# A decoder layer on one core: LAG 7 to 8 in the scan, the first unit's row maxima in two halves, norms of batches 3 and 4 one unit later

## The chip, the core and the metric

One core of a Trainium2 chip computes everything. The metric is device time in microseconds (us) of one launch, as the median of the runs shown. PE is TensorE (PEld its weight loads), DVE VectorE, ACT ScalarE, POOL GpSimd, SP the engine that issues most DMAs.

## What is computed

`x` is four batches of 512 tokens with 256 features, in float32. Three blocks follow each other, each added to `x`:

```python
x = x + mamba(layernorm(x))              # 2 layers; D_INNER 512, 16 states
x = x + cross_attention(layernorm(x), ctx)   # 16 heads of 16, 512 keys
x = x + ffn(layernorm(x))                # shared expert + top 2 of 8
```

A layer of the first block projects to 512 inner channels, runs a convolution of 4 taps and a scan over time with 16 states per channel, and sums the states times C:

```python
v = BETA * v + mi_t
h = dA_t * h + v
y_t = einsum('ben,bn->be', h, C_t)
```

The attention subtracts each query's maximum before the exponential, divides by the sum and projects. The experts follow it and are not touched here.

## The kernel before

**The scan stage.** Two layers of four batches make eight passes, k = 0 to 7, of 64 steps each (16 states by 4 tiles of 128 channels). A step i is one scan of 128x512 on DVE (line 911), which needs its decay from ACT (`dA`, line 1067) and its input from PE (line 704, `v`; PE writes the inputs of two steps at once, at each even step, into two adjoining banks of PSUM). POOL then multiplies the result by C (line 1140), and PE adds it to the sum of its channel tile by four transposes (line 681, `pe_add_state`). PE does this addition LAG steps later: in step i it writes the inputs (if i is even), and then adds state i - LAG. `LAG` is 7 (line 255), and there are LAG + 2 buffers for the states. So PE, in order, can write inputs only when POOL is through with an earlier state.

After its 16th state a channel tile's sum is copied by ACT (line 974, "y"), transposed by PE (line 664, "bt"), combined on DVE (line 828, "xd") and gated on POOL (line 1099). `plan_mid` (line 455) and `plan_back` (line 436) put these pieces at steps that are counted from LAG, while `plan_front` (line 395) puts the pieces of the next pass (projections "p" and "z" line 576, "xp" 586, "dbcT" 595, "d" 600, transposes "u" 614, chunk ends "e1" to "e3" 641) at fixed steps. The convolution's taps are three instructions on DVE (line 799).

**Banks.** Inputs and pieces share six banks (NRING). `banks_for` (line 59) goes through them in PE's order: a piece takes the bank that was used longest ago, an input pair the two adjoining ones used longest ago. PE waits until the bank's last content is read, by a scan (semaphore `scan_done`), by DVE (`bank_dve`) or by ACT (`bank_act`). So which wait stands ahead of an input pair follows from where the pieces stand.

**The attention stage.** It has eight units u (two per batch, 8 heads each) of 16 slots s. Slot s: PE writes the scores of a key tile and two heads into a pair of banks (line 1449, and line 1453 adds the negated maxima by a matmul with `nrow`), ACT takes the exponential of 128x1024 (line 1517), and PE multiplies by the values (line 1470) once for two slots. The maxima themselves come from scores the other way round: PE line 1433, DVE line 1584, 16 of them for each unit. They run four slots ahead (`maxima_at`, line 1328, one per slot). After a unit's 16th maximum `dve_max_parts` (line 1586) splits them in two parts, PE turns them into rows ("rows", line 1400) and DVE copies the rows (line 1562). Scores, maxima and the pieces of `opening` (line 1321) share three pairs of banks in turn; all other pieces ("v", sums, norm, "xn", "q", "out", rows) share a single bank (NONE = 1, line 1289).

`opening` runs ahead of unit 0: the transposes and queries of batch 2 ("xn" line 1386, "q" 1391), unit 0's maxima 4 to 15 (0 to 3 are made earlier), its rows, and maxima 0 to 3 of unit 1. The values "v" of batch 1 (line 1396) are made in slots 0 and 1 of unit 0. Unit 0 also holds, on DVE, the residual sum of batch 3 (`dve_add_x(2)`, line 879), the statistics of batches 3 and 4 (lines 149, 156) and batch 3's scaling (line 171), and on ACT their square root (line 162), for which ACT loads a table and then the exponential's again. Batch 3's "xn" and "q" stand in slots 3, 4, 6 and 8 of unit 1.

## Time and profile before

| | us |
|---|---|
| median of 3 runs | 1496.05 |
| lowest, highest | 1495.28, 1501.35 |
| profiled execution | 1499.4 |
| its span, first to last instruction | 1498.1 |
| 64 steps of the scan stage, 488.80 to 599.50 | 110.7 |
| first to last start of an exponential in attention | 989.4 to 1244.3 |

The stretches of the second group of rows end at the first score of a unit or slot: opening before 988.13, unit 0 from there to 1031.24 (slot 2 starts at 999.71, 6 at 1006.26, 10 at 1014.29), unit 1 to 1063.30; unit 5 is 1165.56 to 1194.09. A busy time is followed by the number of instructions in brackets. A timeline row gives start, duration, engine, line, operation, output<-input, count, and in brackets the idle time ahead of it with the instruction that ended it. Rows of neighbouring instructions are merged. TensorE's granted clock is given as a share of 2.4 GHz: 1.00, or 0.50 for 1.2 GHz. Times in the text are those of the trace's axis, from the start of the span.

### The profile page before, as it was taken

How to read it: one execution, taken by the hardware profiler on the slowest of the kernel's cores; microseconds unless marked ns; L12 is line 12 of the kernel's file. 1: busy time of each engine (PE TensorE's matmuls, PEld its weight loads, DVE VectorE, ACT ScalarE, POOL GpSimd, SP SyncE). 2: the span in 40 equal slices, each digit the busy share in tenths (PEclk: the TensorE clock that was granted, in tenths of full speed). 3: DMA queues.
4: the chain of work that ended last, by engine and by line, in shares of the span. 5: the costliest groups of instructions: out<-in, count | busy, mean ns of one | idle time of the engine just before them, and what ended most of it. 6: DMA issues, size and time to landing. Idle time of an engine off the chain costs nothing.

```text
span 1498.1 us, 47021 instructions
## 1 busy us (share of the span) xinstructions
PE 1365.4 (91%) x20570; PEld 966.3 (65%) x20570; DVE 1054.5 (70%) x1345; ACT 891.2 (59%) x1303; POOL 939.7 (63%) x834
## 2 busy tenths in 40 slices
PE   6999999999999999999999988778998887999997
PEld 3567767767777777776776767433434343589996
DVE  4798788788788788888887888576777751522224
ACT  4767766776776776776776756126565564434440
POOL 1289989889989989989989988540422000044541
PEclk9999999999999999999999999869999999999999
DMA  6322221221321222122122336470725003412215
GB/s 228 148 101 87 87 87 59 87 87 59 115 87 62 84 88 82 63 88 87 62 84 87 111 127 157 94 137 11 131 43 99 0 2 113 177 58 70 70 62 186
DMA packets 44043, 137.38 MB, mean 92 GB/s; under 512 B 9024, under 2 KB 21952, under 8 KB 35008
## 3 DMA queue, kind: packets, MB, share of 16 engines
q1 hardware_dynamic: 37024, 117.85, 24.3%
q0 software_dynamic: 6816, 16.53, 5.0%
q8 instruction: 164, 2.69, 0.7%
q14 instruction: 39, 0.32, 0.1%
HBM read 108.00 MB, written 15.86 MB: 83 GB/s over the span
## 4 chain that ended last, share of the span: by engine, by line
PE 47%; DVE 27%; ACT 12%; issue 9%; DMA 3%; POOL 3%; DVEq 0%; SPq 0%; ACTq 0%; POOLq 0%
DVE hst L911 12%; PE psum L704 7%; PE psum L681 4%; PE psum L1470 4%; PE psum L1878 4%; PE psum L1890 4%; DVE overlay L799 4%; DVE w_early L911 3%; ACT dA L1067 3%; PE psum L641 3%; PE psum L1449 2%; ACT pT L1517 2%; PE psum L576 2%; DMA overlay<-x_hat,origin 2%; PE psum L1433 2%
## 5 line engine op out<-in xcount | busy, mean ns | idle before, releaser
L1140 POOL TENSOR_TENSOR hst<-hst,cb 128x512 f32<-128x512 f32 x399 | 511.2, 1304 | 89.1 <-DVE hst L911 87.1
L911 DVE TENSOR_TENSOR_SCAN hst<-dA,psum 128x512 f32<-128x512 f32 x399 | 464.0, 1203 | 100.8 <-PE psum L704 100.7
L681 PE MATMUL psum<-ident,hst 128*128 128x128 f32 x1596 | 236.9, 282 | 8.1 <-ACT xraw L974 3.6
L1067 ACT ACTIVATE dA<-delta,alog 128x512 f32<-128x512 f32 x256 | 178.1, 718 | 86.6 <-DVE hst L911 67.6
L1067 ACT ACTIVATE dA<-xres,alog 128x512 f32<-128x512 f32 x256 | 176.7, 718 | 69.2 <-DVE hst L911 52.0
L681 PEld LDWEIGHTS psum<-ident,hst 128*128 128x128 f32 x1596 | 174.8, 142 | 57.0 <-issue 20.5
L1584 DVE TENSOR_REDUCE nmax<-psum 128x2 f32<-128x1024 f32 x124 | 150.1, 1221 | 52.6 <-PE psum L1433 51.6
L1517 ACT ACTIVATE pT<-psum 128x1024 f32<-128x1024 f32 x128 | 126.9, 1024 | 92.9 <-PE psum L1453 91.7
L704 PE MATMUL psum<-filt,uT 64*64 64x86 f32 (+1 forms) x6144 | 144.5, 238 | 23.3 <-DVE hst L911 11.5
L704 PEld LDWEIGHTS psum<-filt,uT 64*64 64x64 f32 x6144 | 123.6, 133 | 58.4 <-issue 46.3
L704 PE MATMUL psum<-filt,c_early 64*64 64x86 f32 (+1 forms) x6144 | 143.9, 237 | 18.6 <-DVE hst L911 11.1
L704 PEld LDWEIGHTS psum<-filt,c_early 64*64 64x64 f32 x6144 | 123.2, 133 | 55.7 <-issue 41.7
L1140 POOL TENSOR_TENSOR w_early<-w_early,cb 128x512 f32<-128x512 f32 x113 | 145.7, 1302 | 18.8 <-DVE w_early L911 18.1
L911 DVE TENSOR_TENSOR_SCAN w_early<-dA,psum 128x512 f32<-128x512 f32 x113 | 133.4, 1203 | 32.7 <-PE psum L704 32.7
L2123 POOL DMA_INDIRECT overlay<-x_hat,origin x39 | 37.9, 972 | 185.8 <-DVE c_early L2069 174.2
L576 PE MATMUL psum<-overlay,w_early 128*128 128x512 f32 x256 | 122.6, 606 | 2.8 <-DVE w_early L911 2.0
L2129 POOL DMA_INDIRECT y_choice<-yb,goal x39 | 38.6, 989 | 70.4 <-DVE yb L2083 70.4
L1968 ACT ACTIVATE ht<-psum 128x512 f32<-128x512 f32 x39 | 23.3, 597 | 94.2 <-PE psum L1878 94.2
L1878 PEld LDWEIGHTS psum<-xt,xn 128*128 128x128 f32 x624 | 75.6, 192 | 3.0 <-DVE xt L2075 0.9
L1878 PE MATMUL psum<-xt,xn 128*128 128x128 f32 x624 | 76.1, 275 | 0.7 <-DVE xt L2075 0.7
L799 DVE SCALAR_TENSOR_TENSOR overlay<-psum,w_cv,overlay 128x509 f32<-128x509 f32 (+2 forms) x96 | 71.1, 743 | 6.9 <-ACT overlay L952 4.7
L1890 PE MATMUL psum<-w_down,ht 128*128 x312 | 73.7, 380 | 0.0
(251 smaller groups left out, 2110.8 us busy)
## 6 DMA issues: line engine op xcount, KB each, us to landing
cb<-c_rows SPq DMA_DIRECT2D x64, 1024.0 KB, 4.8
qk_first<-w_early SPq DMA_DIRECT2D x64, 64.0 KB, 2.6
w_up<-up_dram SPq DMA_DIRECT2D x8, 512.0 KB, 7.6
w_down<-down_dram SPq DMA_DIRECT2D x8, 512.0 KB, 13.6
w_up<-y_choice SPq DMA_DIRECT2D x8, 512.0 KB, 7.4
k_kept<-uT SPq DMA_DIRECT2D x3, 1024.0 KB, 5.9
v_kept<-xbs SPq DMA_DIRECT2D x6, 512.0 KB, 2.6
qk<-k_kept SPq DMA_DIRECT2D x48, 64.0 KB, 3.5
```

Of the source, the lines that this page charges most:

```text
L576: i = pe.matmul(bk, w_in[:, kt, m8 * P:(m8 + 1) * P], xnT[:, kt, :], start=kt == 0, stop=kt == KD - 1)
L681: m = pe.matmul(psum[:, Y0 + et % EP, t * P:(t + 1) * P], hst(i)[:, t * P:(t + 1) * P], ident[:], start=n == 0 and t == 0, stop=n == NSTAT ...
L704: m = pe.matmul(halves_at[half][e0:e0 + MT, :, t0:t0 + width], uT[k % 2][r0:r0 + KT, c, et * P + e0:et * P + e0 + MT], filt[r0:r0 + KT, f ...
L799: i = dve.scalar_tensor_tensor(out=dst, in0=bk[:, 0:S - late], scalar=w_cv[:, l, j, tap:tap + 1], in1=dst, op0=ALU.mult, op1=ALU.add)
L911: dve.tensor_tensor_scan(hst(i), a, v, 0.0, ALU.mult, ALU.add).then_inc(scan_done, 1)
L1067: act.activation(dA[:, a % NDA, :], delta[k % 2][:, et, :], ACT.Exp, scale=alog[:, k // B, et, n:n + 1]).then_inc(decay_done, 1)
L1140: pool.tensor_tensor(h, h, cb[:, q % 2, state_of(i)[1] % GN, :], ALU.mult).then_inc(g_done, 1)
L1470: m = pe.matmul(psum[i * HROW:(i + 1) * HROW, PV, :], vt[:, cp, kv, c0:c0 + HROW], pT[:, (m0 + i // 2) % NPT, i % 2, :], start=kv == 0, st ...
L1517: act.activation(pT[:, m % NPT], pair(u, "score", s), ACT.Exp, scale=HDIM ** -0.5).then_inc(pair_act, 1)
L1584: dve.tensor_reduce(nmax[:, u % 2, t, 2 * j:2 * j + 2], pair(u, "max", r), AX.X, ALU.max, negate=True).then_inc(pair_dve, 1)
L1878: m = pe.matmul(psum[:, U0 + j % NUB, ft * P:(ft + 1) * P], wu[:, j % NWU, kt * F + ft * P:kt * F + (ft + 1) * P], xt[:, j % NXT, kt, :], ...
L1890: m = pe.matmul(out_bank(j)[:, 0:D], ht[:, j % NHT, ft, :], w_down[:, bass.ds(at + ft * D, D)], start=ft == 0, stop=ft == FT - 1)
```

## The change

`LAG` becomes 8 (and the state buffers 10). The pieces y, bt, xd and the gates that are counted from LAG come one step later; those of `plan_front` stay. In attention, unit 0's maxima are turned into rows twice: maxima 0 to 7 in the opening (into `nrow[1]`), 8 to 15 in unit 0 (rows at slot 4, used from slot 8 on). The opening ends after maximum 9. Slots 0 to 9 of unit 0 hold two maxima each, all later slots one, so that from the end of unit 0 on they are four slots ahead as before. The residual sum, statistics, root and scaling of batches 3 and 4 go from unit 0 to unit 1 (slots 0 to 6), and batch 3's "xn" and "q" from slots 3, 4, 6, 8 of unit 1 to 7, 8, 10, 12.

```diff
@@ -252,7 +252,7 @@
-            NDA, AHEAD, LAG, NRING, Y0 = 5, 4, 7, 6, 6
+            NDA, AHEAD, LAG, NRING, Y0 = 5, 4, 8, 6, 6
...
@@ -1309,7 +1309,7 @@
-                    for s, name in zip((3, 4, 6, 8), project(b + 2)):
+                    for s, name in zip((7, 8, 10, 12) if u == 1 else (3, 4, 6, 8), project(b + 2)):
...
@@ -1319,23 +1319,27 @@
             opening = project(1)[:2]
-            for r in range(NMX, NSLOT):
+            HALF = NSLOT // 2
+            for r in range(NMX, HALF):
                 opening += [(0, "max", r)] + project(1)[r - NMX + 2:r - NMX + 3 if r - NMX < 2 else 0]
-            opening += [(0, "rows", 0)] + [(1, "max", r) for r in range(AHEAD)]
+            opening += [(0, "max", HALF), (0, "rows", 0), (0, "max", HALF + 1)]
+            to_come = [(0, r) for r in range(HALF + 2, NSLOT)] + [(u, r) for u in range(1, NU) for r in range(NSLOT)]
+            AT_ONCE = [2] * 10 + [1, 1] + [1] * AHEAD
+            slot(0, 4, 0, "rows", 1)
...
             def maxima_at(u, s):
-                if s < NSLOT - AHEAD:
-                    return (u + 1, s + AHEAD) if u + 1 < NU else None
-                return (u + 2, s + AHEAD - NSLOT) if u + 2 < NU else None
+                if u == 0:
+                    return to_come[sum(AT_ONCE[:s]):sum(AT_ONCE[:s + 1])]
+                at = sum(AT_ONCE) + (u - 1) * NSLOT + s
+                return to_come[at:at + 1]
...
-                    if maxima_at(u, s):
-                        v, r = maxima_at(u, s)
+                    for v, r in maxima_at(u, s):
...
@@ -1395,7 +1399,7 @@
-                    pe.wait_ge(max_lo, x + 1)
+                    pe.wait_ge(max_lo, x + 2 if x else j + 1)
...
@@ -1434,6 +1438,9 @@
+            def nrow_at(u, s):
+                return 1 if u == 0 and s < NSLOT // 2 else u % 2
...
@@ -1444,13 +1451,15 @@
+                elif (u, s) == (0, NSLOT // 2):
+                    pe.wait_ge(*taken(u, "rows", 1))
...
-                    m = pe.matmul(o[:, e, :], pick[k0:k0 + KR, j, :], nrow[k0:k0 + KR, u % 2, :], start=False, stop=True, tile_position=(k0, 0))
+                    m = pe.matmul(o[:, e, :], pick[k0:k0 + KR, j, :], nrow[k0:k0 + KR, nrow_at(u, s), :], start=False, stop=True, tile_position=(k0, 0))
...
@@ -1535,7 +1544,7 @@
-                        if s == 9 and u == 0:
+                        if s == 4 and u == 1:
                             act_ln_root(LN2[2], 2 * TB, NT)
...
@@ -1583,16 +1592,17 @@
-            def dve_max_parts(u):
+            def dve_max_parts(u, n, c0, c1):
...
+                dve.wait_ge(*taken(u, "max", 2 * c1 - 1))
+                dve.tensor_copy(hi, maxima).then_inc(max_hi, 1)
+                dve.wait_ge(max_hi, n + 1)
+                dve.tensor_tensor(lo, maxima, hi.bitcast(F32), ALU.subtract).then_inc(max_lo, 1)
...
@@ -1609,8 +1619,8 @@
+                        if (x, j) == (0, HALF - 1):
+                            dve_max_parts(0, 0, 0, HALF // 2)
...
@@ -1618,23 +1628,25 @@
+                        for x in maxima_at(u, s):
+                            dve_max(*x)
+                            if x == (0, NSLOT - 1):
+                                dve_max_parts(0, 1, HALF // 2, UH)
...
+                            dve_max_parts(u + 1, u + 2, 0, UH)
...
+                        if s == 0 and u == 1:
                             dve_add_x(2)
...
+                        if s in (1, 2) and u == 1:
                             dve.wait_ge(x1_done, B)
...
+                            dve_ln_stats(LN2[2], (s + 1) * TB, (s + 2) * TB, xres, s == 2)
+                        if s == 3 and u == 1:
                             dve_ln_aggr(LN2[2], 2 * TB, NT)
...
+                        if s == 6 and u == 1:
                             dve_ln_rec(LN2[2], 2 * TB, NT)
                             dve_ln_scale(LN2[2], 2 * TB, 3 * TB, xres, True)
```

Three places of the order follow. In all, `psum` is the bank written, and the semaphores in brackets are what the instruction waits for.

**PE, last pass (k = 7), around its steps 38 to 40.** `hst` is a state buffer, `filt` and `uT` make a scan's input, `xraw` is the copied sum. Before:

```order
L704 MATMUL psum<-filt,uT 64x2x43 [waits scan_done]
L704 MATMUL psum<-filt,uT 64x2x43 x15
L704 MATMUL psum<-filt,uT 64x2x42 x8
L681 MATMUL psum<-ident,hst 128x128 [waits g_done]
L681 MATMUL psum<-ident,hst 128x128 x3
L681 MATMUL psum<-ident,hst 128x128 [waits y_out,g_done]
L681 MATMUL psum<-ident,hst 128x128 x3
L664 MATMUL psum<-ident,xraw 128x128 [waits y_out,scan_done]
L664 MATMUL psum<-ident,xraw 128x128 x3
L704 MATMUL psum<-filt,uT 64x2x43 [waits scan_done,filt_done]
```

Now:

```order
L681 MATMUL psum<-ident,w_early 128x128 [waits g_done]
L681 MATMUL psum<-ident,w_early 128x128 x3
L704 MATMUL psum<-filt,uT 64x2x43 [waits scan_done,filt_done]
L704 MATMUL psum<-filt,uT 64x2x43 x15
L704 MATMUL psum<-filt,uT 64x2x42 x8
L681 MATMUL psum<-ident,hst 128x128 [waits y_out,g_done]
L681 MATMUL psum<-ident,hst 128x128 x3
L664 MATMUL psum<-ident,xraw 128x128 [waits y_out,scan_done]
L664 MATMUL psum<-ident,xraw 128x128 x3
```

The addition that waits for ACT's copy (`y_out`) stood ahead of the input pair of steps 40 and 41, and stands behind it now.

**PE, pass k = 3, steps 48 to 50**, with the transposes "u" (L614). Before:

```order
L704 MATMUL psum<-filt,uT 64x2x43 [waits scan_done,bank_act,filt_done]
L704 MATMUL psum<-filt,uT 64x2x43 x15
L704 MATMUL psum<-filt,uT 64x2x42 x8
L681 MATMUL psum<-ident,w_early 128x128 [waits g_done]
L681 MATMUL psum<-ident,w_early 128x128 x3
L614 MATMUL psum<-ident,overlay 64x64 [waits u_done,scan_done,bank_act]
L614 MATMUL psum<-ident,overlay 64x64 x31
L681 MATMUL psum<-ident,hst 128x128 [waits g_done]
L681 MATMUL psum<-ident,hst 128x128 x3
L704 MATMUL psum<-filt,uT 64x2x43 [waits scan_done]
```

Now:

```order
L704 MATMUL psum<-filt,uT 64x2x43 [waits bank_act,filt_done]
L704 MATMUL psum<-filt,uT 64x2x43 x15
L704 MATMUL psum<-filt,uT 64x2x42 x8
L681 MATMUL psum<-ident,hst 128x128 [waits g_done]
L681 MATMUL psum<-ident,hst 128x128 x3
L614 MATMUL psum<-ident,overlay 64x64 [waits u_done,scan_done]
L614 MATMUL psum<-ident,overlay 64x64 x31
L681 MATMUL psum<-ident,hst 128x128 [waits g_done]
L681 MATMUL psum<-ident,hst 128x128 x3
L704 MATMUL psum<-filt,uT 64x2x43 [waits bank_act]
```

The two input pairs waited for a scan, and now wait for copies of ACT alone. Odd passes (1, 3, 5) have this order; in the even ones (2, 4, 6) the pair of step 48 still waits for the scan before it.

**DVE, from the end of the mamba stage to slot 2 of unit 0.** TENSOR_REDUCE is a maximum, `nsplit` the parts, `nrow` the rows, `vt` the values. Before:

```order
L1584 TENSOR_REDUCE nmax<-psum 128x2
L1549 SCALAR_TENSOR_TENSOR part<-psum,b_qk,part 128x512
L1584 TENSOR_REDUCE nmax<-psum 128x2 x10
L1593 CAST nsplit<-nmax 128x8x8
L1595 TENSOR_TENSOR nsplit<-nmax,nsplit 128x8x8
L1609 CAST pick<-pT 128x512
L1562 CAST nrow<-psum 128x512
L1584 TENSOR_REDUCE nmax<-psum 128x2 x5
L1557 TENSOR_TENSOR vt<-psum,b_v 128x16x16 x2
```

Now:

```order
L1593 TENSOR_REDUCE nmax<-psum 128x2
L1558 SCALAR_TENSOR_TENSOR part<-psum,b_qk,part 128x512
L1593 TENSOR_REDUCE nmax<-psum 128x2 x2
L1603 CAST nsplit<-nmax 128x8x4
L1605 TENSOR_TENSOR nsplit<-nmax,nsplit 128x8x4
L1593 TENSOR_REDUCE nmax<-psum 128x2
L1619 CAST pick<-pT 128x512
L1571 CAST nrow<-psum 128x512
L1593 TENSOR_REDUCE nmax<-psum 128x2 x3
L1566 TENSOR_TENSOR vt<-psum,b_v 128x16x16 x2
```

The first rows stood behind ten maxima in a row, and stand behind three now.

## Rows read from the trace of the kernel before

**Rows 1.** Page: engines' shares of the chain; the value products (busy us, mean ns).

```profile
PE 47%; DVE 27%; ACT 12%; issue 9%; DMA 3%; POOL 3%; DVEq 0%; SPq 0%; ACTq 0%; POOLq 0%
...
L1470 PE MATMUL psum<-pT,vt 128*32 128x512 f32 x512 | 69.7, 627 | 3.2 <-ACT pT L1517 3.2
```

**Rows 2.** Stretches: length, busy PE, PEld, DVE, ACT, POOL; PEclk, DMA share, GB/s.

```profile
488.80:599.50 110.70, 104.92 (x2204) 79.45 (x2207) 92.65 (x95) 79.07 (x128) 99.94 (x82) 1.00 0.22 80
...
977.00:988.10 11.10, 6.06 (x20) 2.65 (x18) 9.99 (x13) 0.00 (x0) 11.09 (x24) 0.50 1.07 133
988.13:999.71 11.58, 10.55 (x28) 5.82 (x28) 5.83 (x7) 2.05 (x2) 2.22 (x1) 0.58 1.03 239
999.71:1006.26 6.55, 5.71 (x41) 2.42 (x40) 5.15 (x5) 3.88 (x4) 0.00 (x0) 1.00 0.18 55
1006.26:1014.29 8.03, 5.91 (x44) 2.25 (x40) 8.03 (x22) 4.10 (x4) 0.00 (x0) 1.00 0.00 0
1014.29:1031.24 16.95, 13.61 (x81) 5.73 (x77) 11.03 (x17) 9.50 (x10) 0.00 (x0) 0.80 0.00 1
1031.24:1063.30 32.06, 29.98 (x198) 13.22 (x194) 23.01 (x25) 19.92 (x23) 10.12 (x22) 1.00 0.48 77
...
1165.56:1194.09 28.53, 25.00 (x181) 11.35 (x178) 21.71 (x23) 17.39 (x19) 0.00 (x0) 1.00 0.00 1
```

**Rows 3.** Timeline of PE, pass k = 3: input pairs of steps 42 to 50.

```profile
471.92 1.12 PE L704 MATMUL psum<-filt,uT 64*64 64x86 f32 x48 [0.60 <-DVE w_early L911]
...
475.17 1.12 PE L704 MATMUL psum<-filt,uT 64*64 64x86 f32 x48 [1.10 <-DVE xbs L828]
...
483.94 1.12 PE L704 MATMUL psum<-filt,uT 64*64 64x86 f32 x48 [0.36 <-DVE hst L911]
...
487.66 1.12 PE L704 MATMUL psum<-filt,uT 64*64 64x86 f32 x48 [0.33 <-DVE w_early L911]
```

**Rows 4.** Timeline, pass k = 4: an addition waits for POOL; ACT meanwhile.

```profile
502.53 0.42 PEld L681 LDWEIGHTS psum<-ident,hst 128*128 128x128 f32 x4 [0.85 <-POOL hst L1140]
...
501.35 1.95 ACT L1067 ACTIVATE dA<-delta,alog 128x512 f32<-128x512 f32 x3
503.32 1.75 ACT L1029 COPY c_early<-psum 16x512 f32<-16x512 f32 x3
```

**Rows 5.** Timelines of PE and DVE, last pass: waits for POOL, ACT and PE.

```profile
864.10 0.66 PE L681 MATMUL psum<-ident,w_early 128*128 128x128 f32 x4 [1.22 <-POOL w_early L1140]
...
906.03 1.08 PE L681 MATMUL psum<-ident,hst 128*128 128x128 f32 x4 [3.63 <-ACT xraw L974]
...
909.76 1.22 DVE L911 TENSOR_TENSOR_SCAN hst<-dA,psum 128x512 f32<-128x512 f32 x1 [2.54 <-PE psum L704]
```

**Rows 6.** Timelines of DVE and ACT: the opening of attention and the first exponential.

```profile
971.76 11.40 DVE L1584 TENSOR_REDUCE nmax<-psum 128x2 f32<-128x1024 f32 x10
...
984.98 0.69 DVE L1562 CAST nrow<-psum 128x512 fp32r<-128x512 f32 x1 [0.94 <-PE psum L1400]
...
989.39 1.02 ACT L1517 ACTIVATE pT<-psum 128x1024 f32<-128x1024 f32 x1 [18.33 <-PE psum L1453]
```

**Rows 7.** Timelines of ACT and PE around the root in unit 0.

```profile
1015.03 1.28 ACT L162 ACT_TABLE_LOAD   x1
...
1019.03 0.80 PE L1433 MATMUL psum<-qk_first 64*128 64x512 f32 x2 [3.10 <-ACT pT L1517]
...
1022.66 0.80 PE L1449 MATMUL psum<-qk_first 64*128 64x512 f32 x2
...
1024.11 0.63 PE L1449 MATMUL psum<-qk_first 64*128 64x512 f32 x2
```

**Rows 8.** Timeline of DVE: residual sum, statistics, a query part.

```profile
1005.13 1.22 DVE L879 TENSOR_TENSOR xres<-xres,xm 128x1024 f32<-128x1024 f32 x1
...
1007.39 1.39 DVE L149 BATCH_NORM_STATS2 stat<-xres 128x6 f32<-128x256 f32 x4
...
1045.75 0.75 DVE L1549 SCALAR_TENSOR_TENSOR part<-psum,b_qk,part 128x512 fp32r<-128x512 f32 x1 [1.49 <-ACT part L1504]
```

27 lines of the change are left out of this document (7 added, 20 removed).

## The prediction

> **What bounds the kernel now.** I read the page first, then the chain of waits, then stretches. The page says that no engine alone is the bound: the chain lies 47% on PE, 27% on DVE, 12% on ACT and only 3% on POOL [rows 1]. That already says something on LAG: a later addition gives POOL more time, and POOL is almost never what is last. In one pass of 110.7 us PE is busy for 104.9, DVE for 92.7 and POOL for 99.9 [rows 2]; PE and DVE hand the chain to and fro through the six banks. The places where PE waits for DVE ahead of an input pair are in [rows 3], the one where it waits for POOL in each pass is in [rows 4]. Attention: in the opening the first exponential comes after ACT was idle for 18.33 us, while DVE makes ten maxima in 11.40 us [rows 6]. PE is busy for 6.06 of 11.10 us there, at a granted clock of 0.50, so 1.2 GHz [rows 2]. The units that follow are bound by PE: unit 5, which has no projection, takes 28.53 us, or 3.57 for two slots; unit 1 with a projection takes 32.06 [rows 2].
>
> **Part 1, LAG 8: the waits for POOL.** PE waits 0.85 us for POOL once a pass. With LAG 8 that wait goes, since POOL is then asked for the state before. But ACT is in one row of work at that time, without a gap, from 501.35 on [rows 4], and DVE's next scans wait for ACT's decays: the wait is hidden, and I take 0 for it (bounds 0 and -0.85 for each of 7 passes, -6). In the last pass POOL is really last, since two gates and filters stand in its queue; PE waits 1.22 us [rows 5]. What PE needs next, the output projection, needs the last gate, which POOL now does one state later than before, so POOL's end there does not move. Only one addition of PE (0.66) goes out of its way: -0.5.
>
> **Part 2, LAG 8: other banks for the input pairs.** This is the part that counts. Since bt and xd move by a step and the fixed pieces don't, `banks_for` hands the banks out differently. Working its rule through for the six full passes:
> - Odd passes (1, 3, 5). Before, the pairs of steps 42, 48 and 50 need the scan just before them, and step 44's needs DVE's xd. PE waits 0.60, 0.36, 0.33 and 1.10 us there, 2.39 together [rows 3]. Now the pair of 42 needs a copy of ACT, 44's an xd two steps back, and 48's and 50's copies of ACT (the second place of the order). All of it could go, -2.4. DVE is only partly idle there, and the stretch after it hangs on ACT's copies of u and e1, so I take -1.5 (bounds -2.4 and 0).
> - Even passes (2, 4, 6). Step 44 no longer waits for xd, but for scan 43, and 46 and 48 wait as before; 50 waits for ACT only. That is worth -0.3 to -0.6; I take -0.5.
> - In all six, xd of channel tile 2 now stands behind a scan more, and the pair of step 10 waits for it: +0.2 by counting DVE's row (a scan of 1.22 [rows 5] against PE's 1.12 for a pair [rows 3]), bounds 0 and +0.6.
>
> Sum: 3 x -1.5 + 3 x -0.5 + 6 x 0.2 = -4.8.
>
> **Part 3, LAG 8: the last pass.** At step 39 PE adds the first state of a channel tile and waits 3.63 us for ACT's copy; the input pair of step 40 stands behind it, and DVE is idle for 2.54 us [rows 5]. Now the pair stands ahead (first place of the order), so these 2.54 us go. ACT's copy comes one decay (1.95 / 3 = 0.65 [rows 4]) later, which the two scans in hand cover. I take -2.5 (bounds -3 and 0). After that POOL runs without a gap to the end of the stage, and it had been waiting for DVE before, so it can start earlier by as much.
>
> **Part 4, the opening.** Before, the rows are copied at 984.98 [rows 6]. Now maxima 6 to 8 stand ahead of them instead of 6 to 15. Three maxima at 1.14 (11.40 / 10) from 971.76 are over at 975.2; parts and the copy of `pick` come between, as before: from the last maximum's end, 983.2, to the rows' end, 985.7, it was 2.5; one of the three maxima now falls into the wait in it, which saves 0.8. So the rows are done at 975.2 + 2.5 - 0.8 = 976.9. PE's first score was also behind four maxima of unit 1, and started at 988.1; now it stands directly behind the rows and maximum 9, at 977.0. -11.1 us (bounds -10 and -11.5).
>
> **Part 5, unit 0.** The ten maxima that left the opening are in slots 0 to 9.
> - Slots 0 and 1 took 11.58 us at clock 0.58, with the four products that make the values through the one bank [rows 2]. One more maximum each is about 0.3 of a slot's 1.45 at 1.2 GHz [rows 7], so 0.4: +0.9, together 12.5.
> - Slots 2 to 9. The nearest stretch without other work, slots 2 to 5, takes 6.55 for four slots, 3.28 for two [rows 2]. With four maxima for two slots DVE alone needs 4.56, and because PE's value products (69.7 / 64 = 1.1 for two slots [rows 1]) stand in order between a maximum and the next score, I take 4.86 (an estimate; bounds 4.56 and 5.4). Times 4, and 1.0 for parts and rows: 20.5. Slots 10 to 15 have one maximum: as in unit 5, 11.9.
> - Together 44.9 us, against 43.1 before (988.13 to 1031.24): +1.8. It would be more, but the work that leaves unit 0 had cost there: in slots 6 to 9, 8.03 us instead of 6.55, and from slot 10 on 16.95 instead of 11.9 (root, and the clock at 0.80 behind it) [rows 2, 7].
>
> **Part 6, unit 1.** It took 32.06 us at clock 1.00 [rows 2]. Added are:
> - on DVE 1.22 (sum), 2 x 1.39 (statistics) [rows 8], and by estimate from these some 0.6 (aggregation) and 1.6 (reciprocal, scaling). In slots 0 to 3 that is 4.6 on top of four maxima of 1.14 and one group's sums: 9.5 or less for DVE where PE needs 4 x 28.53 / 16 = 7.1 by unit 5: +2.0.
> - on ACT the root between two table loads of 1.28. PE waited 3.10 behind them in unit 0 [rows 7], and will in unit 1: +3.0, with 2.5 more if the clock falls behind it as it did there (that is in the bounds).
> - "xn" of batch 3 in slot 7 waits for the scaling that ends in slot 6: +0.8. "q" in slots 10 and 12 now has sums (11) and rows (13) directly behind it on the single bank, which is free only after ACT's part and DVE's; DVE's takes 0.75 after a wait of 1.49 for ACT's [rows 8]. Two maxima and scores of cover leave +0.6 each, 1.2.
> - less 0.6, as DVE catches up while PE waits for ACT.
>
> Sum +6.4 (bounds +3 and +9). Of the queues: strips of batch 3 leave SP and POOL some 8 us later, and are first needed in slot 12 of unit 3, 60 us later: 0. ACT's root also waits for DVE's aggregation one slot before, as before.
>
> **The sum.** Mamba: -0.5 - 4.8 - 2.5 = -7.8. Attention: -11.1 + 1.8 + 6.4 = -2.9. Together -10.7 against the profiled 1499.4 us (span 1498.1), so about 1488.7 for a profiled run. The median of the runs is 3.4 below that run: 1496.05 - 10.7 = 1485.4.
>
> **A rule that speaks against it.** In slots 6 to 9 of unit 0 PE is busy for only 5.91 of 8.03 us and keeps the clock at 1.00; from 1014.29 on it is 0.80 on average, behind a wait of 3.10 us [rows 2, 7]. The Trainium skill, "TensorE: Matmul & The Clock Gate", section "A second HAM failure mode: psum-queue depth-cycling", says that short idle times between groups of matmuls, as PSUM buffers are gone through in turn, are enough to make the clock go to and fro. Unit 0 will have just such idle times. By the row the sum stays; by the rule it is the third rival below.
>
> **The rivals.**
> - *Only the last pass and attention gain* (chance 0.24). What speaks for it: DVE is busy for 92.7 of 110.7 us in a pass, and after step 50 comes a chain over e1, e2 and e3 that ACT's copies set, so PE's waits may be mere slack. Then part 2 is 0 or +1: 1490 to 1493, with the last pass absorbed as well 1494.
> - *Attention gains more* (0.16). If the root's 3 us fall into the time in which DVE is behind anyway, and the clock comes up earlier since PE is dense from 975 on, unit 1 costs +3 and unit 0 takes 42: 6 less, 1479.
> - *The clock stays at 1.2 GHz in units 0 and 1* (0.06). For it: the idle times of about 0.7 us for two slots in slots 2 to 9, where PE waits for DVE. Against it: slots 6 to 9 at 1.00 [rows 2]. Price: score, its row and a maximum take 1.45 us [rows 7] instead of half of that, the value products 2.2 instead of 1.1 [rows 1]; that is 0.8 more for two slots where DVE is the bound, and 1.6 where PE is: some +9 in unit 0 and +12 in unit 1, 1506 in all, slower than before. It decides if the clock stays down for more than 13 slots; as long as it falls only behind the root, as now, it is in the sum.
> - *The change doesn't do what it says:* the scores could start at 977 and be held by something else. The banks in turn give every score of slots 0 to 9 the pair that the score before had, so it waits for that exponential. A round of score, exponential (1.02 [rows 6]) and two hand-overs is 2.3 us, below DVE's 2.4 for a slot. If it is above, +0.3 for each of 8 slots: 1488. That is within my case's range.
>
> **How the numbers follow.** My case has 0.50 (1481 to 1489), the rivals 0.24, 0.16 and 0.06, and 0.04 is left for something between (the LAG parts making the scan stage longer while attention gains, 1496 to 1500). The predicted time is my case's, 1485.4. The range takes in the first rival and most of the second: 1478 to 1495. A difference of 0.5%, 7.5 us, is about what a measurement of this kernel can tell from no change; faster by more than that is below 1488.6: 0.46 of my case and the second rival, 0.62. Slower than 1503.5: 0.04. Within: 0.34.
>
> **What would show it.** Passes k = 1, 3, 5 about 1.5 us shorter than the even ones, where they are equal now; no wait for DVE ahead of PE's pairs of 48 and 50. No idle DVE in the last pass ahead of the scan of step 40. The first exponential some 15.5 us after the opening's first instruction instead of 26.5 (989.39 on today's axis, 978.3 then, less what the mamba stage gains). Unit 0 near 45 us, bound by DVE, at clock 1.00 from slot 2 on; unit 1 near 38 us with PE waiting for ACT in slots 5 and 6. I am wrong if odd and even passes stay equal, if unit 0 is above 50 us, or if units 2 to 7 change at all, which nothing here should move.

## The result, and the profile after

The changed kernel takes 1487.65 us (median of 7 runs, 1486.05 to 1491.99), the one before 1496.05: a ratio of 0.9947, 95% interval 0.9928 to 0.9965, so 8.4 us faster where I had said 10.7. Its profiled run took 1486.92 us, with a span of 1485.6; the span is 12.5 shorter than that of before. The sum was nearly right, the terms were not: the full passes gained more and the last pass nothing, the opening gained more, and unit 1 lost almost twice what I had put down for it.

The page of the changed kernel: busy time of the engines, and the chain of waits by engine, beside [rows 1].

```profile
PE 1361.3 (92%) x20574; PEld 966.7 (65%) x20574; DVE 1055.1 (71%) x1348; ACT 892.2 (60%) x1303; POOL 938.6 (63%) x834
...
PE 50%; DVE 25%; ACT 11%; issue 8%; DMA 2%; POOL 2%; SPq 1%; DVEq 0%; ACTq 0%
```

SPq, the queue of SyncE, was at 0% of the chain before and is at 1% now; the last pass will show why. The stretches of the changed kernel (length, busy PE, PEld, DVE, ACT, POOL; granted clock, DMA share, GB/s): passes k = 3 and 4, the last pass up to attention's opening, the opening, unit 0 whole and in three parts, unit 1 whole and in four.

```profile
372.74:482.59 109.85, 104.95 (x2205) 79.71 (x2201) 92.82 (x95) 79.21 (x129) 99.98 (x82) 1.00 0.24 84
482.59:593.13 110.54, 104.83 (x2204) 79.58 (x2200) 92.72 (x95) 79.20 (x129) 99.92 (x82) 1.00 0.24 85
812.28:954.65 142.37, 127.35 (x2376) 99.95 (x2372) 111.90 (x122) 76.21 (x117) 113.60 (x93) 0.94 0.43 120
954.65:967.38 12.73, 8.99 (x34) 4.18 (x34) 8.67 (x12) 2.45 (x4) 9.25 (x13) 0.86 0.69 166
967.38:1009.33 41.95, 34.55 (x210) 16.09 (x210) 35.50 (x39) 16.65 (x17) 13.27 (x24) 0.96 0.60 114
967.38:977.67 10.29, 8.12 (x32) 5.01 (x32) 6.85 (x8) 2.05 (x2) 10.29 (x22) 0.84 1.06 154
977.67:997.46 19.79, 15.69 (x101) 6.42 (x101) 18.91 (x20) 8.20 (x8) 2.98 (x3) 1.00 0.71 161
997.46:1009.33 11.87, 10.74 (x82) 4.66 (x78) 9.74 (x12) 6.41 (x7) 0.00 (x0) 1.00 0.00 0
1009.33:1053.77 44.44, 35.33 (x196) 15.38 (x192) 28.66 (x47) 23.14 (x26) 9.56 (x20) 0.85 0.25 39
1009.33:1016.90 7.57, 4.41 (x30) 2.66 (x26) 6.53 (x11) 3.55 (x4) 0.00 (x0) 0.88 0.00 1
1016.90:1026.99 10.09, 8.05 (x42) 3.34 (x42) 5.50 (x15) 6.93 (x8) 0.00 (x0) 0.75 0.01 2
1026.99:1035.60 8.61, 6.53 (x30) 2.83 (x26) 4.78 (x8) 3.16 (x4) 4.08 (x8) 0.60 0.79 122
1035.60:1053.77 18.17, 16.34 (x99) 6.55 (x98) 11.84 (x15) 9.50 (x11) 5.48 (x12) 1.00 0.23 36
```

A pass is measured here from PE's first e1 product (step 50) to the same of the next. So read, the 12.5 us divide as follows: the opening of attention starts at 954.65 and not at 962.93 (-8.3), it lasts 12.73 to the first score and not 25.20 (-12.5), unit 0 41.95 and not 43.11 (-1.2), unit 1 44.44 and not 32.06 (+12.4), unit 2 33.67 and not 34.86 (-1.2), unit 6 +0.7, and what follows the last score is 2.6 shorter. That last item belongs to nothing: over all 14 profiled kernels of this study this part takes 250.7 to 256.4 us, in no relation to the edits. Unit 2's is no sure part either: nothing of it is edited, and it takes 33.7 us in five of the ten kernels with attention's change and about 35 in the other nine.

The same division for every kernel that ran (us, one profiled execution each; "scores" is the opening's start to the first score). The ratios are against the kernel before on the same chip, where its median was between 1495.9 and 1498.5, so kernels are compared by their ratios and not by their medians. Kernels that share a stage, such as the last passes of the change and of lag_alone, show how much one execution says of it.

| kernel | median | ratio (95%) | k = 3 | k = 4 | last pass | scores | unit 0 | unit 1 |
|---|---|---|---|---|---|---|---|---|
| before | 1496.05 | | 111.5 | 110.8 | 141.9 | 25.2 | 43.1 | 32.1 |
| the change | 1487.65 | 0.9947 (0.9928-0.9965) | 109.9 | 110.5 | 142.4 | 12.7 | 42.0 | 44.4 |
| lag_alone | 1487.48 | 0.9927 (0.9898-0.9956) | 109.2 | 110.5 | 142.5 | 25.4 | 43.3 | 32.1 |
| att_alone | 1497.95 | 0.9994 (0.9975-1.0014) | 111.2 | 110.8 | 141.9 | 13.9 | 43.6 | 43.3 |
| pieces_alone | 1487.01 | 0.9941 (0.9916-0.9967) | 109.7 | 110.7 | 143.8 | 25.5 | 43.3 | 32.1 |
| adds_alone | 1497.26 | 1.0007 (0.9989-1.0026) | 112.3 | 111.1 | 142.6 | 25.4 | 43.3 | 32.1 |
| aq_later | 1483.10 | 0.9899 (0.9867-0.9930) | 108.9 | 110.6 | 137.5 | 13.9 | 43.5 | 41.2 |
| ln_later | 1484.53 | 0.9911 (0.9880-0.9941) | 109.7 | 110.5 | 141.6 | 14.1 | 42.1 | 38.2 |
| halves_norms_back | 1484.33 | 0.9922 (0.9898-0.9946) | 108.6 | 110.5 | 142.4 | 12.7 | 51.2 | 32.1 |
| root_as_identity | 1484.62 | 0.9916 (0.9886-0.9946) | 109.7 | 110.5 | 141.9 | 12.7 | 43.5 | 40.5 |
| both_later | 1478.31 | 0.9883 (0.9859-0.9907) | 109.0 | 110.5 | 137.0 | 13.9 | 43.6 | 39.3 |
| even_as_odd | 1481.39 | 0.9890 (0.9858-0.9921) | 108.7 | 109.9 | 136.1 | 12.7 | 42.0 | 38.3 |
| xn_later | 1476.52 | 0.9868 (0.9838-0.9897) | 108.9 | 110.5 | 138.7 | 12.7 | 43.6 | 35.2 |
| even_last_bo | 1469.47 | 0.9822 (0.9791-0.9853) | 108.8 | 108.1 | 138.3 | 14.4 | 43.7 | 35.2 |

### The profile page after: what moved, and what is told of

It reads as the page before. It is cut to its first block, busy times and chain, and to the rows that moved or that the text cites. A ratio compares the mean times of both kernels' runs of the same rounds, so it can differ in the third digit from the quotient of the medians.

```text
span 1485.6 us, 47034 instructions
## 1 busy us (share of the span) xinstructions
PE 1361.3 (92%) x20574; PEld 966.7 (65%) x20574; DVE 1055.1 (71%) x1348; ACT 892.2 (60%) x1303; POOL 938.6 (63%) x834
## 4 chain that ended last, share of the span: by engine, by line
PE 50%; DVE 25%; ACT 11%; issue 8%; DMA 2%; POOL 2%; SPq 1%; DVEq 0%; ACTq 0%
DVE hst L911 11%; PE psum L704 7%; PE psum L681 5%; PE psum L1479 4%; PE psum L1890 4%; PE psum L1902 4%; DVE overlay L799 4%; ACT dA L1067 3%; PE psum L576 3%; DVE w_early L911 3%; PE psum L641 3%; PE psum L1458 2%; ACT pT L1526 2%; PE psum L1832 2%; DVE nmax L1593 2%
## 5 line engine op out<-in xcount | busy, mean ns | idle before, releaser
L1140 POOL TENSOR_TENSOR hst<-hst,cb 128x512 f32<-128x512 f32 x410 | 523.8, 1300 | 87.9 <-DVE hst L911 85.8
L911 DVE TENSOR_TENSOR_SCAN hst<-dA,psum 128x512 f32<-128x512 f32 x410 | 475.4, 1203 | 100.9 <-PE psum L704 100.9
L681 PE MATMUL psum<-ident,hst 128*128 128x128 f32 x1640 | 242.7, 283 | 5.1 <-ACT xraw L974 2.6
L681 PEld LDWEIGHTS psum<-ident,hst 128*128 128x128 f32 x1640 | 180.4, 142 | 55.9 <-issue 24.7
L1526 ACT ACTIVATE pT<-psum 128x1024 f32<-128x1024 f32 x128 | 127.0, 1024 | 84.9 <-PE psum L1462 83.1
L704 PE MATMUL psum<-filt,uT 64*64 64x86 f32 (+1 forms) x6144 | 145.1, 238 | 17.9 <-DVE hst L911 11.2
L704 PE MATMUL psum<-filt,c_early 64*64 64x86 f32 (+1 forms) x6144 | 143.5, 237 | 18.6 <-DVE hst L911 11.5
L1140 POOL TENSOR_TENSOR w_early<-w_early,cb 128x512 f32<-128x512 f32 x102 | 131.5, 1305 | 12.4 <-DVE w_early L911 11.7
L911 DVE TENSOR_TENSOR_SCAN w_early<-dA,psum 128x512 f32<-128x512 f32 x102 | 119.6, 1202 | 20.7 <-PE psum L704 20.7
L2141 POOL DMA_INDIRECT y_choice<-yb,goal x39 | 38.5, 986 | 68.2 <-DVE yb L2095 68.2
L1479 PE MATMUL psum<-pT,vt 128*32 128x512 f32 x512 | 71.8, 644 | 2.5 <-ACT pT L1526 2.5
```

The source lines that it names most:

```text
L681: m = pe.matmul(psum[:, Y0 + et % EP, t * P:(t + 1) * P], hst(i)[:, t * P:(t + 1) * P], ident[:], start=n == 0 and t == 0, stop=n == NSTAT ...
L704: m = pe.matmul(halves_at[half][e0:e0 + MT, :, t0:t0 + width], uT[k % 2][r0:r0 + KT, c, et * P + e0:et * P + e0 + MT], filt[r0:r0 + KT, f ...
L911: dve.tensor_tensor_scan(hst(i), a, v, 0.0, ALU.mult, ALU.add).then_inc(scan_done, 1)
L1140: pool.tensor_tensor(h, h, cb[:, q % 2, state_of(i)[1] % GN, :], ALU.mult).then_inc(g_done, 1)
L1479: m = pe.matmul(psum[i * HROW:(i + 1) * HROW, PV, :], vt[:, cp, kv, c0:c0 + HROW], pT[:, (m0 + i // 2) % NPT, i % 2, :], start=kv == 0, st ...
L1526: act.activation(pT[:, m % NPT], pair(u, "score", s), ACT.Exp, scale=HDIM ** -0.5).then_inc(pair_act, 1)
```

## Experiments 1 and 2: one half of the change alone

```
lag_alone, against before:
-            NDA, AHEAD, LAG, NRING, Y0 = 5, 4, 7, 6, 6
+            NDA, AHEAD, LAG, NRING, Y0 = 5, 4, 8, 6, 6
att_alone: the changed kernel with this line as before
```

> The kernel before with LAG = 8 and nothing else. Between the traces of before and after, the opening of attention starts 8.3 us earlier (962.93 to 954.65), and all of that should be LAG's: about 1488 us, odd passes (k = 1, 3, 5) 1.6 to 2.2 shorter than the 110.75 of before, even ones 0.2, the last pass (from its first L641 to the opening) unchanged near 142. Attention's units as before (43.1, 32.1). Rival: part of the 8.3 comes from what stands behind (code and data placed otherwise), then this kernel is at 1491 or above.

> The changed kernel with LAG = 7: attention's part of the change alone. By the traces of before and after: opening -12.5, unit 0 -1.2, unit 1 +12.4, unit 2 -1.2, so -2.4, and the opening's start at 962.9 as before: about 1493.5 us. Behind attention 2.6 us were also gone in the changed kernel; if they belong to attention's edits they show here too (1491), if to LAG's in the run of LAG alone, if in neither they are spread of one execution.

LAG alone gives all that was measured: 0.9927, with the passes of the changed kernel and attention as before. Attention's half gives nothing that can be measured, 0.9994: from the opening's start to the last score it takes 279.4 us against 280.3 before. The opening gained 11.3 and unit 1 gave back 11.2.

## Experiments 3 and 4: is it the banks or POOL?

LAG moves two things at once: PE's additions, and the pieces that the planner counts from LAG (y, bt, xd, output). Each can be moved alone. In pieces_alone all pairs and pieces stand in the very banks of the changed kernel, in adds_alone in those of before; for both this is exact: `banks_for`, given their orders, hands out the same banks pair for pair.

```
pieces_alone, against before:
-                    plan_back(k - 1, k, LAG - 2)
+                    plan_back(k - 1, k, LAG - 1)
-                    s = EP * NSTATE + LAG - 2 * EP + 2 + 2 * e
+                    s = EP * NSTATE + LAG + 1 - 2 * EP + 2 + 2 * e
adds_alone, against before: LAG = 8, and the two lines with LAG - 3 and LAG - 1
```

> The kernel before with PE's additions seven states later as they were, but y, bt, xd, gate and output pieces of plan_back and plan_mid one step later, where LAG = 8 puts them. The input pairs and pieces then have the very banks that LAG = 8 gives them. Theory (part 2 of the prediction): the scan stage gains by the banks, so odd passes (k = 1, 3, 5) are at 108.6 to 109.9 us and even ones at 110.5, as with LAG alone (108.63, 109.15, 108.64), and the whole is 1489 to 1491. Rival: the gain is that PE's additions no longer wait for POOL (0.85 us in each pass); then all passes stay at 110.75 and the whole at 1498.

> The kernel before with LAG = 8 for PE's additions alone: the pieces of plan_back and plan_mid stay at the steps, and all pairs and pieces in the banks, of LAG = 7. The counterpart of pieces_alone. By the theory passes stay at 110.75 and the whole is 1498 (the last pass 0 to -0.5); y of a channel tile may then wait one state for its last addition, up to +1 for each of the passes. By the rival the passes are at 109 to 110 each and the whole is near 1489.

The pieces carry the gain (0.9941), the later additions have none (1.0007) and cost 2.1 us over six passes. (The profiled run of pieces_alone is the slowest of its eight, 1495.99 us, so its trace shows less of the gain than the median does.) The timeline of PE in pass k = 3 shows where it comes from, pairs of steps 40 to 50. First pieces_alone, the pairs from step 42 on:

```profile
468.12 1.12 PE L704 MATMUL psum<-filt,uT 64*64 64x86 f32 x48
470.63 1.12 PE L704 MATMUL psum<-filt,uT 64*64 64x86 f32 x48
475.66 1.12 PE L704 MATMUL psum<-filt,uT 64*64 64x86 f32 x48
478.98 1.12 PE L704 MATMUL psum<-filt,uT 64*64 64x86 f32 x48
482.29 1.12 PE L704 MATMUL psum<-filt,uT 64*64 64x86 f32 x48
```

Then adds_alone, from step 40 on: the waits of [rows 3] are all there, to the hundredth of a microsecond.

```profile
466.69 1.12 PE L704 MATMUL psum<-filt,uT 64*64 64x86 f32 x48 [0.33 <-DVE w_early L911]
471.80 1.12 PE L704 MATMUL psum<-filt,uT 64*64 64x86 f32 x48 [0.60 <-DVE hst L911]
475.04 1.12 PE L704 MATMUL psum<-filt,uT 64*64 64x86 f32 x48 [1.10 <-DVE xbs L828]
480.07 1.12 PE L704 MATMUL psum<-filt,uT 64*64 64x86 f32 x48
483.81 1.12 PE L704 MATMUL psum<-filt,uT 64*64 64x86 f32 x48 [0.36 <-DVE w_early L911]
487.53 1.12 PE L704 MATMUL psum<-filt,uT 64*64 64x86 f32 x48 [0.33 <-DVE hst L911]
```

The two halves do not simply add. Over the six passes k = 1 to 6 adds_alone is 2.1 us longer than before, pieces_alone 6.2 shorter, and with both it is 8.1 shorter. Once the pairs don't hold PE, the later additions seem to be worth something: the eight kernels with the six passes of the change take 657.6 to 659.3 us for them, and pieces_alone 660.6. But that is one execution, and in the time of the whole the intervals of pieces_alone and lag_alone overlap.

Was the wait for POOL of [rows 4] hidden, as I had it, or was it none? The same place in the changed kernel, weight loads and then matmuls:

```profile
496.41 0.42 PEld L681 LDWEIGHTS psum<-ident,hst 128*128 128x128 f32 x4 [0.85 <-POOL w_early L1140]
...
495.44 1.04 PE L641 MATMUL psum<-c_early,overlay 64*16 64x512 f32 x6
496.42 0.66 PE L681 MATMUL psum<-ident,hst 128*128 128x128 f32 x4
```

The 0.85 us are still there with LAG 8, and in adds_alone and pieces_alone too. They are idle time of the weight loads alone: the matmuls of L641 run meanwhile (495.44 to 496.48), and the addition follows them without a gap. In the kernel before it was the same, 501.56 to 502.60. So no wait of PE stood there that a later addition could have removed.

One thing the two kernels don't separate: the banks and the steps of the pieces always move together. That the banks do it rests on the waits. In odd passes those of steps 42, 44, 48 and 50 are gone, the four that the plan lets start earlier; in even passes that of step 50 is, while 44 and 48 keep theirs. Only the wait of step 42 is gone in even passes too, where the plan doesn't say so.

## Experiment 5: where the gain of the last pass went

The last pass takes 142.37 us, 0.4 more than before. The wait of 3.63 us of [rows 5] is now one of 2.62, DVE is no longer idle ahead of the scan of step 40, and up to step 46 the pass has kept 2.3 us: ACT is ready for the copy of the first query piece 96.8 us after the pass's start (before: 99.1). Then this stands in SP's queue and on ACT in the changed kernel:

```profile
895.06 9.77 SPq L1218 DMA_DIRECT2D qk_first<-w_early  x14
904.88 0.58 SPq L1158 DMA_DIRECT2D cb<-c_rows  x1
905.50 3.85 SPq L1222 DMA_DIRECT2D qk_first<-w_early  x6
...
908.72 5.46 DMA qk_first<-w_early
...
914.20 0.69 ACT L1047 ACTIVATE w_early<-psum,b_qk 128x512 fp32r<-128x512 f32 x1 [5.13 <-DMA qk_first<-w_early]
```

SP moves the keys of batch 1 in 32 strips of 64 KB out of the rows of `w_early` into which ACT's copy of the first query piece (aq, step 47) goes. The first 12 of them start at 885.25, and SP starts one every 0.70 us (14 in 9.77). The last is issued at 908.72 and lands 5.46 us later (the row from the chain of waits), at 914.2; the median of the 32 is 2.9. Ahead of the last six stands a load of 1024 KB (`cb`, 904.88) in the same queue. So both the row of issues, 24 us long, and the slow landing behind that load are in the limit, and no run here separates them. ACT stands still for 5.13 us, and DVE, whose scans need its decays, for 4.38. In the trace of before the wait is 1.81 us (921.91, ACT): the strips were the limit there already. Against the start of the pass they start at the same time in both (73.0 us), and the last lands at 101.9 instead of 100.9. So 5.13 is the 1.81 of before, the 2.3 that were gained ahead of it, and 1.0 for the later landing. The edit puts the query pieces three steps later, over the time that the strips need.

```
aq_later, against the changed kernel:
-                    put(46 + j, "pe", "aq", j)
-                    put(47 + j, "act", "aq", j)
-                    put(47 + j, "dve", "aq", j)
+                    put(49 + j, "pe", "aq", j)
+                    put(50 + j, "act", "aq", j)
+                    put(50 + j, "dve", "aq", j)
```

> The changed kernel with the two early query pieces of the last pass (aq) at steps 49 and 50 instead of 46 and 47. Theory: the 2.5 us that I forecast for the last pass were gained up to step 47 and given back there, because ACT's copy of aq overwrites the rows from which SP still moves 32 strips of keys (5.13 us of wait at 914.20, before 1.81). Then the wait falls below 1 us, and the stage ends 2 to 4 us earlier: 1484 to 1485.5. Rival: POOL's gates, with 4.7 us of idle time there but none behind it, end the stage anyway: then below 1 us, 1487 +- 0.5. A second rival: the query strips leave SP later and PE's first maxima wait for them, +1.

The wait in aq_later:

```profile
912.55 0.69 ACT L1047 ACTIVATE w_early<-psum,b_qk 128x512 fp32r<-128x512 f32 x1 [2.16 <-DMA qk_first<-w_early]
```

I had expected it below 1 us, and it is 2.16; the last pass falls from 142.37 to 137.48, by 4.9 instead of 2 to 4. Of these, 3.0 are the shorter wait and 1.0 a shorter idle time of DVE at step 42 (0.74 instead of 1.77), which I had not foreseen; 0.9 come behind the last scan. All five kernels with this edit have a last pass of 136.1 to 138.7 us, all nine without it one of 141.6 to 143.8. The whole is at 0.9899, and its interval overlaps that of the change by 0.0002, so the gain is shown by the stage and not by the time of the kernel. The strips bound this stretch, and a gain ahead of them is lost unless the piece behind them moves as well. The Trainium skill, "DMA: Bandwidth & Descriptors", section "Issuing engines are not separate DMA queues", says that the time on the sequencer to start a DMA is usually small relative to the DMA itself. For a single strip the trace agrees: 0.61 us to issue (median of the 14), against 2.9 from issue to landing. But 32 of them in one queue add up: they take 9.14, 9.77 and 3.85 us to issue, 23 us of the stage.

## Experiments 6 to 8: unit 1

PE in unit 1 of the changed kernel, its waits of over 0.5 us, and the DVE rows that the first of them hangs on.

```profile
1015.90 1.09 PE L1412 MATMUL psum<-ident,w_early 128*128 128x128 f32 x4 [2.74 <-DVE w_early L1581]
...
1026.65 0.50 PE L1437 MATMUL psum<-qk 64*128 64x512 f32 x2 [1.80 <-ACT pT L1526]
...
1030.15 1.09 PE L1390 MATMUL psum<-ident,xm 128*128 128x128 f32 x4 [2.08 <-DVE xm L171]
```

```profile
1011.47 1.22 DVE L879 TENSOR_TENSOR xres<-xres,xm 128x1024 f32<-128x1024 f32 x1
1012.61 1.22 DVE L1593 TENSOR_REDUCE nmax<-psum 128x2 f32<-128x1024 f32 x1
1013.74 1.40 DVE L149 BATCH_NORM_STATS2 stat<-xres 128x6 f32<-128x256 f32 x4
1015.05 0.24 DVE L1577 RECIPROCAL rc<-psum 128x16 f32<-128x16 f32 x1
1015.33 0.42 DVE L1581 TENSOR_TENSOR w_early<-psum,rc 128x256 f32<-128x256 f32 x1
```

The transposes of slot 2 ("norm", L1412) need the sums of unit 0, which DVE divides only after the residual sum and the first statistics. PE stands for 2.74 us. The clock falls to 0.50 around it, comes back, and falls once more behind the wait for the root, in that for the scaling; the stretches above have means of 0.75 and 0.60, and it is at 1.00 for good only from 1035.60 on. The same unit in aq_later has the same wait of 2.74 us, but the clock falls only once, behind the root, and it takes 41.21 us:

```profile
1006.20:1047.41 41.21, 32.54 (x197) 14.01 (x193) 28.31 (x47) 23.00 (x26) 9.64 (x20) 0.92 0.26 42
```

```
ln_later, against the changed kernel:
-                    for s, name in zip((7, 8, 10, 12) if u == 1 else (3, 4, 6, 8), project(b + 2)):
+                    for s, name in zip((9, 10, 12, 14) if u == 1 else (3, 4, 6, 8), project(b + 2)):
-                        if s == 4 and u == 1:
+                        if s == 6 and u == 1:
                             act_ln_root(LN2[2], 2 * TB, NT)
-                        if s == 0 and u == 1:
+                        if s == 2 and u == 1:
                             dve_add_x(2)
and two slots later in the same way: statistics 3, 4, aggregation 5, reciprocal and scaling 8
halves_norms_back: the same lines as in the kernel before (unit 0; projections 3, 4, 6, 8 of unit 1)
root_as_identity, against the changed kernel:
-                            act_ln_root(LN2[2], 2 * TB, NT)
+                            act.wait_ge(ln_aggr, LN2[2])
+                            act.activation(stat[:, 2 * TB:NT, 8], stat[:, 2 * TB:NT, 7], ACT.Identity, bias=epst[:, 0:1]).then_inc(ln_root, 1)
```

> The changed kernel with the norm work of batches 3 and 4 two slots later in unit 1: sum in slot 2, statistics in 3 and 4, aggregation 5, root 6, reciprocal and scaling 8, projections in slots 9, 10, 12, 14. Theory: unit 1 took 44.4 us and not 38.5, since DVE's sum and statistics stand ahead of the row sums of unit 0, which PE's transposes (norm) wait 2.74 us for, and the granted clock falls to 0.5 behind that and two more waits of 1.8 and 2.1. With DVE's new work behind the row sums that first wait goes and the clock stays at 1.00 until the root: unit 1 near 39, 1482 in all. Rival: the clock falls behind the root and the wait for the scaling as well, only later, unit 1 stays at 43 to 45: 1487.

> The changed kernel with the norm work of batches 3 and 4 back in unit 0 (slots 4 to 12) and the projections at slots 3, 4, 6, 8 of unit 1, as before; LAG 8 and the maxima in two halves stay. It tells apart whether moving the norms paid. Unit 1 should be back at 32.1 (44.4 in the changed kernel); unit 0, where ten maxima and the norm work of DVE (some 6.5 us with the scaling) now meet, goes from 41.9 to 41.9 + 6.5 + 3 for the root = 51 or more: 12.3 less against 9.5 more, 1485 (bounds 1482 and 1490). Rival: with two maxima a slot DVE is so late in unit 0 that its clock stays at 1.2 GHz, unit 0 takes 58, 1492.

> The changed kernel with the root of the norms of batches 3 and 4 replaced by a plain copy with bias on ACT (so the scaling is by 1/(variance + eps), part of the computation left out): all waits stay, ACT's two table loads of 1.28 us go. Theory: the root is one of three causes of unit 1's 44.4 us, PE waits 1.80 us behind it and the granted clock is 0.60 to 0.75 from the first of these waits on. Unit 1 then takes 40 to 42, the whole 1484 to 1485. Rival: the waits for DVE (2.74 and 2.08) set the unit alone and hide the root: 44 and 1487. A second rival: the root with the clock behind it is nearly all of it, 37 and 1480.

Waits of PE of over 0.5 us in unit 1 of ln_later:

```profile
1014.04 0.63 PE L1412 MATMUL psum<-ident,w_early 128*128 128x128 f32 x4 [0.55 <-DVE w_early L1581]
...
1022.23 0.50 PE L1458 MATMUL psum<-qk_first 64*128 64x512 f32 x2 [1.47 <-DVE nmax L1593]
...
1025.60 0.50 PE L1437 MATMUL psum<-qk 64*128 64x512 f32 x2 [0.77 <-ACT pT L1526]
1029.04 0.63 PE L1390 MATMUL psum<-ident,xm 128*128 128x128 f32 x4 [2.02 <-DVE xm L171]
```

2.74 has become 0.55, and the transposes take 0.63 and not 1.09, so the clock is up. A new wait of 1.47 us has come: DVE's work now stands ahead of a maximum. The unit takes 38.2 us, 39.3 and 38.3 in both_later and even_as_odd, where it is the same, against 44.4, 43.3 and 41.2 in the three kernels with the order of the change. So the order on DVE is worth 1.9 to 6.2 us, of which 1.8 are PE's waits in the traces of the change and of ln_later (2.74 against 0.55 + 1.47, 1.80 against 0.77, 2.08 against 2.02); what is more goes with the clock. That 38.2 is close to the 38.5 of my prediction is chance: I had 3.0 for the root there and nothing for this. With the norms back in unit 0 the two units take 51.22 + 32.06 = 83.3 us against 86.4 in the changed kernel and 80.3 in ln_later: where the change put the norms they cost more than where they were, two slots further on less. The two units of the other kernels keep to that order (86.9 and 84.7 with the norms where the change has them, 82.9 and 80.2 two slots on), but for the norms in unit 0 there is one trace only. The medians (0.9922, 0.9947, 0.9911) stand in that order, but their intervals overlap. Of the root I learn less. Without its table loads the wait of 1.80 us is one of 0.39 to 0.42, and the unit takes 40.5; but the same unit with the root takes 44.4, 43.3 and 41.2 in three kernels in which nothing of it differs (the change, att_alone, aq_later; granted clock 0.85, 0.88, 0.92). So the root is worth between 0.7 and 4 us there, and its size stays open.

## Experiments 9 and 10: both, and the wait that is left

```
both_later: the edits of aq_later and of ln_later in one kernel
xn_later, against both_later:
-                    for s, name in zip((9, 10, 12, 14) if u == 1 else (3, 4, 6, 8), project(b + 2)):
+                    for s, name in zip((10, 12, 14, 15) if u == 1 else (3, 4, 6, 8), project(b + 2)):
```

> The changed kernel with the query pieces of the last pass three steps later and the norm work of batches 3 and 4 two slots later, the two edits of aq_later and ln_later together. They lie in different stages, -4.9 us in the last pass (142.4 to 137.5) and -6.2 in unit 1 (44.4 to 38.2) by the traces; if they add, 1487.65 - 4.9 - 6.2 = 1476.6, if only as the medians of the two runs say (ratios 0.9899 and 0.9911 against 0.9947), 1496 x 0.985 = 1474 to 1482. Rival: the clock's fall in unit 1 comes in other executions at other places, and the gain of the one is lost: 1483.

> both_later with the projections of unit 1 at slots 10, 12, 14, 15 instead of 9, 10, 12, 14: in both_later PE waits 2.02 us ahead of the transposes of slot 9 for DVE's scaling, and 4 us at a granted clock of 0.74 follow. Theory: that wait goes, unit 1 from 39.3 to 36.5 to 37.5, the whole 1476. Rival: the last projection at slot 15 keeps the single bank from the row sums in slot 1 of unit 2, and the gain is lost there: unit 2 2 us longer, 1478.

The edits of aq_later and ln_later together give 0.9883 (1478.3; I had 1476.6). The last pass takes 137.0, unit 1 39.3. The wait of 2.02 us at slot 9 is in this kernel too. xn_later moves the projections to slots 10, 12, 14 and 15: the wait is gone, unit 1 is at a clock of 1.00 throughout and takes 35.17 us, in the row below (less than the 36.5 to 37.5 expected), and unit 2 is not longer than in aq_later (35.05 against 35.16). I can't say where the 1.3 us and more beyond the expected gain come from, other than that the clock does not fall at all. even_last_bo has the same unit, and takes 35.18. The whole: 0.9868; against both_later that is within the intervals.

```profile
1005.27:1040.44 35.17, 30.41 (x197) 13.08 (x194) 28.14 (x47) 23.00 (x26) 3.85 (x8) 1.00 0.19 31
```

## Experiments 11 and 12: the even passes

Odd passes are at 108.6 to 109.9, even ones at 110.5. The banks' order comes out differently in them: by the plan three pairs of an odd pass need the scan just ahead of them, six of an even one. In the trace of the changed kernel two of these, of steps 44 and 48, wait for it in even passes (1.14 and 0.36 us) and none in odd ones. If that is the cause, one output piece elsewhere in even passes makes them odd.

```
even_as_odd, against both_later:
-                    s = s + 1 if at == "last" else ((17, 19, 21, 23) if at == NI - 1 else (19, 25, 29, 34))[t]
+                    s = s + 1 if at == "last" else ((17, 19, 21, 23) if at == NI - 1 else (19, 25, 27 if at % 2 == 0 else 29, 34))[t]
even_last_bo, against xn_later: (19, 25, 29, 38 if at % 2 == 0 else 34)
```

> both_later with one more edit: in passes k = 2, 4, 6 the third output piece of the pass before (bo 2) goes at step 27 instead of 29, so that the banks' order of an odd pass repeats. By the table of banks, pairs that may not start before the scan just ahead of them is through are 3 in each pass then (steps 24, 26, 46); in the changed kernel odd passes have these 3 and take 108.6 us, even ones have 6 (24, 26, 42, 44, 46, 48) and take 110.5, and before each pass had 6 and took 110.75. Theory: those pairs set the length of a pass; even passes fall to 108.6, three times -1.9, and the whole to 1478.3 - 5.7 = 1472.6. Rival: an odd pass is short because the even one before it has done part of its work (or leaves it behind); then both kinds settle between, 109.6 or 110.5 each, and the whole stays within 1 us of 1478.

> xn_later with the last output piece of the pass before (bo 3) at step 38 instead of 34 in passes k = 2, 4, 6. It gives even passes the same banks as even_as_odd did (pairs of steps 24, 26, 46 behind the scan just ahead), but leaves DVE's row up to step 34 as it is. In even_as_odd the waits of 1.14 us at step 44 and 0.36 at step 48 were gone, as the banks say, and a new one of 1.81 stood at step 38, where ACT's roots came 1.4 us later behind the piece that I had moved. Theory: without that, even passes take 110.5 - 1.14 - 0.36 - 0.3 = 108.6 to 109.1, and the whole is 1476.5 - 3 x 1.6 = 1471.7. Rival: even passes are held by ACT's row of table loads and roots at steps 36 to 42 whatever the banks are; the waits only move, passes stay at 110 to 110.5 and the whole at 1475 to 1477.

even_as_odd fell short: 110.65, 109.89 and 110.36 for k = 2, 4, 6, where 108.6 was expected, and 0.9890, no better than both_later. But the waits of 1.14 and 0.36 us at steps 44 and 48 were gone, and one had come at step 38, next to the row in which ACT makes its roots. PE in pass k = 4 of even_as_odd:

```profile
569.24 1.12 PE L704 MATMUL psum<-filt,c_early 64*64 64x86 f32 x48 [1.81 <-DVE hst L911]
```

even_last_bo gives the same banks by moving a piece that stands behind that place. The even passes k = 2 and 4, with k = 3 between them:

```profile
261.75:370.22 108.47, 105.14 (x2204) 79.57 (x2201) 91.75 (x95) 79.18 (x129) 99.01 (x81) 1.00 0.22 78
370.22:478.97 108.75, 104.95 (x2204) 79.70 (x2200) 92.63 (x95) 79.23 (x129) 100.67 (x83) 1.00 0.25 91
478.97:587.09 108.12, 104.79 (x2205) 79.50 (x2200) 91.75 (x95) 79.18 (x129) 99.30 (x81) 1.00 0.21 79
```

They are 2.1 and 2.4 us shorter than in the changed kernel, k = 6 1.4, and the whole is at 0.9822 (1469.5 us; 1471.7 expected). That is the fastest of all; against the changed kernel it is some 1.3% (0.9822 / 0.9947), by ratios taken on different chips, and its interval overlaps that of xn_later, so that the 5.6 us of this edit are those of the traces. The waits at steps 44 and 48 of the even passes are gone, and one of 0.77 at step 40 with them: 2.3 us in all, about as much as k = 2 and 4 are shorter. PE's waits ahead of the pairs set the length of a pass, and the plan of the banks says where they stand, provided that the move that gives them doesn't delay a scan by itself. Here too the piece and the banks moved together.

## Why the prediction was right, and where not

The time was in the range and near its middle, 1487.65 against 1485.4, by terms that were off by up to 6 us and mostly cancelled. That part is luck.

- **Part 1, no gain from the waits for POOL: the number right, the reading wrong.** adds_alone, in which only PE's additions are later, is at 1.0007. But the wait of 0.85 us does not go with LAG 8, as I had written, and is not hidden by ACT's work: [rows 4] is a row of PEld, and PE's matmuls run meanwhile.
- **Part 2, other banks: the mechanism right, the size too small.** -8.1 over six passes, where I had -4.8. Odd passes are 2.6, 1.6 and 2.2 us shorter, where I had 1.3 each: nearly all of the 2.39 us of waits, of which I had written "all of it could go" and then took 1.5, for a slack that is not there. The failed step is this discount: PE is busy for 105 of 110 us, and what its waits lose the pass loses. (The pair of step 40 waits 0.77 us now and 0.34 before, so that the waits are 1.96 shorter in all.) Even passes are 1.3, 0.2 and 0.2 shorter, where I had 0.3 each. The wait for xd at step 10 is there in even passes alone, 0.31 us, where I had 0.2 in all six. The first rival (mere slack) is out. One execution each: against att_alone, whose scan stage is that of before, it is -7.3 and not -8.1.

Pairs of step 40 of k = 3 and step 10 of k = 4 in the changed kernel:

```profile
463.03 1.12 PE L704 MATMUL psum<-filt,uT 64*64 64x86 f32 x48 [0.77 <-DVE w_early L911]
...
519.31 1.12 PE L704 MATMUL psum<-filt,c_early 64*64 64x86 f32 x48 [0.31 <-DVE xbs L828]
```

- **Part 3, the last pass: wrong.** -3.0 with part 1's share, measured +0.4. The 2.54 us did go, and 2.3 of them were still there at step 47. The step that failed is to count them for the whole stage: I followed DVE to step 40 and not past the next thing that doesn't move with it, the 32 strips in SP's queue. The trace of before had it, with 1.81 us of wait at 921.91. Nor does POOL run without a gap from there to the end of the stage: it is idle for 4.70 us ahead of 916.95, behind DVE.
- **Part 4, the opening: the mechanism right, the size outside its bounds (-10 to -11.5).** -12.5 here and -10.8 to -12.5 in the other kernels, predicted -11.1; the granted clock was 0.86 there and is 0.77 to 0.81 in the kernels at -11. The first exponential comes 13.98 us after the opening's first instruction, predicted 15.5.
- **Part 5, unit 0: +1.8 predicted, -1.2 measured; of the eight other kernels with this unit two are at -1.0 and -1.2, six at +0.3 to +0.6.** Slots 2 to 15 are as worked out (19.79 and 11.87, predicted 20.5 and 11.9; 21.2 to 21.3 for slots 2 to 9 where the clock falls, see the third rival). The term that was off is slots 0 and 1: 10.29 and not 12.5, since the clock is at 0.84 and not at 0.58 there, as the second rival had it. It is 10.3 to 10.5 in all but even_last_bo (12.06, clock 0.67).
- **Part 6, unit 1: +6.4 predicted (bounds 3 and 9), measured +12.4, and +9.1 and +11.3 in the two other kernels with the same unit.** I had counted DVE's work, and the queue of DVE in slots 0 to 3 with "one group's sums" in it, but not who waits for these sums: PE's transposes in slot 2, ahead of every later score. That is the step that failed. The clock fell there, and again behind the root. Of the waits that I had, the root's was 1.80 and not 3.0, and that of "xn" for the scaling 2.08 and not 0.8. With the first wait down to 0.55 the unit takes 38.2 to 39.3.
- **The third rival**, the clock: part of it came. In slots 2 to 9 of unit 0 of the changed kernel PE waits up to 0.66 us at a time (1.50 once, in slots 0 and 1), is busy for 15.69 of 19.79 us and keeps 1.00. But nine kernels have these slots, and in five of them (att_alone, aq_later, root_as_identity, both_later, xn_later) the clock falls to 0.50 for 3.4 us in the middle, with the same waits, and the slots take 21.2 to 21.3 us. Below is the row of att_alone, where it falls at 1001.5, behind a wait of 0.63 us. The Trainium skill, "TensorE: Matmul & The Clock Gate", section "A second HAM failure mode: psum-queue depth-cycling", says that such short idle times, as PSUM buffers are gone through in turn, make the clock go to and fro. In the trace of the change slots 2 to 9 don't show it; over nine traces five do, for 1.4 us and not for the +9 of the rival. What decides between the two is not shown. In unit 1 it falls in all three kernels with this unit, once or twice.

```profile
987.44:1008.65 21.21, 17.28 (x101) 6.90 (x100) 18.90 (x20) 8.19 (x8) 2.80 (x2) 0.92 0.61 146
```

- The fourth rival (scores held by exponentials) shows in two waits, 0.66 us at 979.52 and 0.52 at 994.47, and decides nothing.
- Of the signs of being wrong, one came: unit 2 is 1.2 us shorter. It is so in five of the ten kernels with attention's change and in none of the four without, so it may come with the change in some executions; the cause is open. Odd and even passes do differ, and unit 0 is below 50 us.

## What to carry to other kernels

Where buffers are handed out by a planner, one moved piece changes who empties the buffer of every piece behind it: compare the waits that the new order makes, and separate the two (same order, other time; other order, same time) before either is credited. A wait in a row of weight loads is not yet a wait of PE: look at what the matmuls do meanwhile. A gain in the middle of a stage is counted only up to the next thing that doesn't move with it; look for the waits for transfers that are already there, even short ones. And work that is put on an engine with time to spare goes behind what another engine is about to ask of it: two slots were worth 1.9 to 6.2 us here.

## What I had not expected of the hardware

- SP issues a transfer of 64 KB in 0.61 us (median of the 14 that took 9.77) and starts one every 0.70, and 32 of them in a row, the last landing 5.46 us after its issue, were the limit of a stretch of the last pass, in which PE is busy for 127.35 of 142.37 us: ACT stood for 5.13 us, and DVE behind it for 4.38.
- The granted clock at the start of attention differs between kernels in which the stretch is the same: the opening takes 12.7 us (clock 0.86 to 0.88) or 13.9 to 14.4 (0.77 to 0.81), unit 0 42.0 to 42.1 or 43.5 to 43.7, unit 1 41.2 to 44.4. The two don't go together: xn_later has the short opening and 43.6, ln_later the long one and 42.1. One profiled execution prices an edit of 1 to 3 us in such a place only together with others.
